# The transposes of the probabilities, moved to stand directly behind the scores on TensorE

## The reference, cut to what matters

```
x = x + scan_block(layernorm(x))             # a state-space scan with 16 states
x = x + cross_attention(layernorm(x), ctx)   # 32 heads of 128
x = x + ffn(layernorm(x))                    # one 512 x 512 matrix and low-rank terms
```

```
h  = layernorm(x);  hn = rmsnorm(h) * ln_weight
q, k, v = hn @ w_q.T, ctx @ w_k.T, ctx @ w_v.T
score = q k^T + position_bias[h]          # masked keys: minus infinity
prob  = softmax(score)
out   = (prob v) @ w_out.T                # summed over the 32 heads
result = h + out
```

## Time and profile before

| | us |
|---|---|
| median of 3 runs | 909.33 (909.28 to 910.69) |
| the profiled execution, its own time | 907.23 |
| its span, first to last instruction | 905.4 |
| TensorE busy | 896.5 (99%) |
| VectorE busy | 694.7 (77%) |
| GpSimd busy | 670.8 (74%) |
| ScalarE busy | 520.2 (57%) |

### The profile page before, as it was taken

How to read it: one execution, slowest core, us unless ns; L and a number is a source line. 1 busy time by engine, 2 the same in 40 slices (tenths; PEclk the granted TensorE clock), 3 DMA queues, 4 the chain that set the end, 5 groups by cost and what they waited for, 6 DMA issues and landing times.

```text
span 905.4 us, 15443 instructions
## 1 busy us (share of the span) xinstructions
PE 896.5 (99%) x5146; PEld 776.4 (86%) x5146; DVE 694.7 (77%) x757; ACT 520.2 (57%) x1198; POOL 670.8 (74%) x437
## 2 busy tenths in 40 slices
PE   8999999999999999999999999999999999999998
PEld 7687888788888888888899999999899999999876
DVE  4799899999999997475666767676667676767774
ACT  3787867665666765456555555555555555555330
POOL 3245989997678795566788787888987878787522
PEclk9999999999999999999999999999999999999999
DMA  9454767576686762457445444444454544444302
GB/s 304 174 168 146 201 200 207 185 216 207 193 281 191 240 198 96 145 172 243 161 147 161 137 158 143 152 146 153 131 166 135 160 136 160 140 156 138 98 1 94
DMA packets 96913, 150.32 MB, mean 166 GB/s; under 512 B 10608, under 2 KB 35312, under 8 KB 96736
## 3 DMA queue, kind: packets, MB, share of 16 engines
q1 hardware_dynamic: 86496, 131.60, 44.4%
q10 hardware_dynamic: 10368, 18.09, 7.7%
HBM read 113.88 MB, written 35.78 MB: 165 GB/s over the span
## 4 chain that ended last, share of the span: by engine, by line
PE 85%; POOL 7%; DVE 4%; issue 2%; DMA 1%; ACT 1%; SPq 0%; ACTq 0%; DVEq 0%; POOLq 0%
PE acc L522 10%; PE acc L524 10%; PE acc L523 10%; PE misc L522 6%; PE misc L523 6%; PE misc L524 6%; PE acc L754 6%; PE acc L809 6%; PE acc L686 5%; PE acc L688 5%; PE acc L687 5%; PE acc L778 3%; POOL y L1538 2%; POOL wv_lo L1500 2%; DVE misc L1268 1%
## 5 line engine op out<-in xcount | busy, mean ns | idle before, releaser
L1538 POOL TENSOR_TENSOR y<-y,w 128x2048 f32<-128x2048 f32 x31 | 143.5, 4629 | 34.9 <-DVE w L1275 31.1
L1268 DVE TENSOR_TENSOR_SCAN misc<-dA,misc 128x2048 f32<-128x2048 f32 x32 | 141.7, 4429 | 4.9 <-ACT dA L881 1.7
L1120 ACT ACTIVATE prob<-prob,negm 128x128 f32<-128x128 f32 x256 | 99.9, 392 | 43.6 <-DVE negm L1336 43.6
L1127 ACT ACTIVATE ot_hi<-acc 128x512 fp32r<-128x512 f32 x64 | 38.3, 599 | 143.5 <-PE acc L809 143.5
L1602 POOL TENSOR_TENSOR wt_lo<-ws,wt_hi 128x1024 fp32r<-128x1024 f32 x27 | 65.2, 2414 | 61.6 <-ACT wt_hi L1108 59.4
L522 PE MATMUL misc<-wo_hi,ot_hi 128*128 128x512 f32 x256 | 107.3, 419 | 0.0
L522 PE MATMUL acc<-wv_hi,ctx_hi 128*128 128x512 f32 x256 | 100.4, 392 | 1.4 <-POOL wv_lo L1500 1.4
L524 PE MATMUL misc<-wo_hi,ot_lo 128*128 128x512 f32 x256 | 101.2, 395 | 0.0
L523 PE MATMUL misc<-wo_lo,ot_hi 128*128 128x512 f32 x256 | 101.1, 395 | 0.0
L1619 POOL TENSOR_TENSOR wo_lo<-wo_raw,wo_hi 128x512 fp32r<-128x512 f32 x64 | 95.9, 1499 | 6.3 <-ACT wo_hi L1084 6.3
L524 PE MATMUL acc<-wv_hi,ctx_lo 128*128 128x512 f32 x256 | 99.8, 390 | 0.0
(11 more groups left out here) (206 smaller groups left out, 2448.2 us busy)
## 6 DMA issues: line engine op xcount, KB each, us to landing
k_scratch<-kst SPq DMA_DIRECT2D x64, 256.0 KB, 3.7
bc<-xp_scratch ACTq DMA_DIRECT2D x32, 512.0 KB, 5.6
v_scratch<-vst SPq DMA_DIRECT2D x32, 512.0 KB, 3.6
k_sb<-k_scratch SPq DMA_DIRECT2D x64, 256.0 KB, 2.7
v_sb<-v_scratch SPq DMA_DIRECT2D x64, 256.0 KB, 2.7
wo_raw<-in_wo SPq DMA_DIRECT2D x64, 256.0 KB, 2.9
wp<-in_wq SPq DMA_DIRECT2D x54, 256.0 KB, 3.7
wraw<-in_wk SPq DMA_DIRECT2D x32, 256.0 KB, 4.8
```

The costliest lines, as they stand in the source:

```text
L1120: last = act.activation(prob[q][:, b], prob[q][:, b], ACT.Exp, bias=negm[q][:, b:b + 1], accum_out=psum[q][:, b:b + 1])
L1268: dve.tensor_tensor_scan(h_ps, flat(dA[k % 2][:, :, :, :]), h_ps, 0.0, ALU.mult, ALU.add).then_inc(da_free, 1)
L1538: pool.tensor_tensor(y_half(half), y_half(half), w[:, k % 2], ALU.add).then_inc(y_ready, 1)
```

## The change

In TensorE's `step` the block with the transposes (with its two waits) moves from behind the products S1 and W11 to directly behind the scores. No instruction is added or taken away, and no other engine's program differs.

```diff
@@ in step(g, par, half, i) of the tensor engine @@
                     mm.then_inc(s_done, 1)
+                if runs(g - 2):
+                    pe.wait_ge(p_ready, g - 1)
+                    if known(g) and g == 2:
+                        pe.wait_ge(sum_evac, slot(NG, 0) - 1)
+                    else:
+                        pe.wait_ge(ot_lo_done, g - 2)
+                    for b in range(HB):
+                        mm = pe.transpose(psT[:, b * S:(b + 1) * S], prob[p][:, b], ident[:])
+                    mm.then_inc(t_done, 1)
                 if paired(i) and not p:
                     pe.wait_ge(c11_done, count(i))
                     product(sumX, S1, pp, *t_of(half, T1), True).then_inc(p5_done, 1)
                 if p and paired(i + 1):
 ...
                     pe.wait_ge(wa_lo, count(i) + 1)
                     product(sumX, W11, 1 - pp, *z_of(of, 0, 0), True).then_inc(p1_done, 1)
-                if runs(g - 2):
-                    pe.wait_ge(p_ready, g - 1)
-                    if known(g) and g == 2:
-                        pe.wait_ge(sum_evac, slot(NG, 0) - 1)
-                    else:
-                        pe.wait_ge(ot_lo_done, g - 2)
-                    for b in range(HB):
-                        mm = pe.transpose(psT[:, b * S:(b + 1) * S], prob[p][:, b], ident[:])
-                    mm.then_inc(t_done, 1)
                 if known(g) and STEPS <= g <= STEPS + 1:
```

## The result

| | before | after |
|---|---|---|
| median of 20 runs each, us | 909.07 (907.12 to 910.91) | 910.72 (909.14 to 912.68) |
| span of the profiled execution, us | 905.4 | 909.0 |
| first product with v, start of its first weight load in the trace, us | 392.95 | 394.81 |
| last product with v, the same, us | 871.31 | 874.90 |
| between these two, us | 478.36 | 480.09 |

The ratio is 1.0019, 95% interval 1.0011 to 1.0026, so 1.0 to 2.4 us slower. The forecast was 911.7, 2.3 us slower than the 909.33 it started from.

The account below looks back on a forecast made before the run. TensorE, busy 896.5 of 905.4 us, was taken as the bound. Its own work changing by 0, 26 waits of 0.09 us add 2.3 to 909.33: 911.7 us, own range 910.6 to 913.2, 8-in-10 range 909.8 to 914.0.

Parts of the forecast that it names:

- TensorE's own work: TensorE's matmuls in the new order: 0 to 0.5 us faster over 54 steps, taken as 0.
- Rival 3: f32/fp32r changes on TensorE really cost 0.08 us; 54 blocks save 4.3 us, less 2.3 of waits: 907.3 us; 5%.
- seams: Places on TensorE where one kind of matmul block follows another; claimed to cost 0.00 to 0.01 us each.
- Even steps: Transposes ahead of S1 in 27 steps: `ot_lo` is done 0.85 us earlier, so no wait.
- A wait for `ot_lo` in 26 odd steps: Transposes ahead of W11, steps 11 to 61: each waits 0.09 us for `ot_lo`, 2.3 us together.
- The three terms: One odd-step wait: `ot_lo` late 0.03, its end to the load 0.11, less 0.05 free: 0.09 us.
- What W11's delay triggers: W11 ends 0.53 us later, ScalarE's exponentials start 0.08 later; no second wait at S2.
- a thin margin at c21: Free time between `c21_done` and S2's load: 0.07 us, staying about 0.08 as TensorE itself arrives 0.09 later.
- Rival 2: Exponentials slip more than TensorE, `c21_done` misses S2 in each even step: 912.4 to 919.2 us, middle 915; 10%.
- The reaction to a semaphore: From `ot_lo`'s end to the transposes' load: 0.11 us taken, 0.05 kept as lower end; the skill gives 50-100 ns.

Follow-up runs that it names:

- e1: Kernel before with the transposes moved directly behind the scores in even steps alone; odd steps keep them behind W11. Ratio to the kernel before 0.9998.
- e5: Changed kernel with `ot_lo` computed in four pieces of 128 columns. Ratio to the kernel before 1.0067.
- e3: Changed kernel with the wait for `p_ready` moved ahead of the scores, so the transposes' first load waits for `ot_lo` alone. Ratio to the kernel before 1.0014.
- e8: Changed kernel with the transposes' two waits in the other order, `ot_lo_done` first and `p_ready` second. Ratio to the kernel before 1.0000.
- e7: Changed kernel with the W11 block moved ahead of the scores in odd steps. Ratio to the kernel before 1.0005.
- e9: Changed kernel with GpSimd's `wo_lo` put ahead of its `bm`. Ratio to the kernel before 1.0027.
- e2: Kernel before with the transposes moved directly behind the scores in odd steps alone; even steps keep them behind S1. Ratio to the kernel before 1.0027.

## Why the prediction was right

The mechanism and the place were right; the size was 0.6 us too large. The time, 910.72, lies 1.0 us below the forecast and just inside its own range of 910.6 to 913.2: 0.3 of this is the kernel before, whose median came out at 909.07 and not 909.33. The forecast gave "slower by over 0.2%" 0.58 and "within 0.2%" 0.36; the ratio of 1.0019 is narrowly in the second.

- **TensorE's own work, taken as 0.** Right to 0.01 us: e1 shows 0.006 to 0.013 us won in each even step, 0.28 us in all, inside the 0 to 0.5 that was kept as a bound. Rival 3, dear seams, is out by the same run.
- **Even steps have 0.7 us and more of cover.** Right: e1 loses nothing, and e5 makes `ot_lo` 0.19 us later without a loss there.
- **A wait for `ot_lo` in 26 odd steps.** Right in place and count. The three terms: `ot_lo` late by 0.03 (measured 0.026 in the first steps, 0.034 later); from its end to the load 0.11 (0.115, and e3 and e8 show that 0.06 of it is the order of the waits); 0.05 of a late load free (the second transpose 0.17 behind the load, 0.22 in a dense stream). An odd step grew by 0.078 to 0.101 us, forecast 0.09; 26 of them by 2.34, forecast 2.3.
- **What made the total smaller than forecast**, 1.73 and not 2.3 in the trace: the 0.3 us of the seams, taken as 0, 0.3 us given back where TensorE had waited before and now arrives later, and 0.07 in step 9. The last two were not in the sum at all.
- **What W11's delay triggers.** Nothing, as forecast. The first links held: the copy of W11 came 0.53 us later (forecast 0.53) and the exponentials 0.08 (forecast 0.08). But the margin at the end was kept by something that the prediction did not have, so that part was luck. It passed ScalarE's 0.08 us on through the normalisation with its length fixed, to a thin margin at c21. In fact the normalisation's end, and c21 behind it, was tied to the end of GpSimd's `bm`. Step 31 after, answering to the earlier trace rows: `bm` ends at 616.06 and the normalisation 0.56 us later, at 616.62; c21 ends at 617.01 and S2's load comes 0.155 us behind it, where it was 0.117 before. The normalisation takes 1.37 us and not 1.44. In most even steps the load comes 0.155 behind c21 (0.11 to 0.13 before); with 0.05 for the wait, the free time before S2 rose from 0.07 to 0.10 us.

```profile
614.90 1.16 POOL L1615 TENSOR_TENSOR bm<-bias,maskadd 128x512 f32<-128x512 f32 x1
...
615.25 1.37 DVE L1360 TENSOR_TENSOR prob<-prob,rec 128x512 f32<-128x512 f32 x1
616.59 0.42 DVE L1369 TENSOR_TENSOR q_sb<-acc,q_s 128x256 f32<-128x256 f32 x1
...
617.17 0.19 PEld L686 LDWEIGHTS acc<-tz,wt_hi 128*128 128x128 f32 x1
```

Rival 2 was priced with a length of VectorE that can't be carried over; e7, which delays the exponentials by 0.7 us at no cost, shows the margin to be far from thin on that side.
- **The reaction to a semaphore.** With the late wait on the load itself the runs show 0.053 us, with it in the second place 0.115. The Trainium skill (Advanced Engine Details and Errata, Network/Comms) gives 50-100 ns: the first agrees, the second lies just outside, and the row of the same instruction was the better guide.

## What to carry to other kernels

Before a consumer is moved ahead on a saturated engine, look at when its last input is ready against the new place, to the hundredth: cover of 0.7 us was worth nothing beyond the first 0.1, but its absence was paid 26 times. Of two waits on one load, write first the one that comes last, and check in the trace that it is on the load itself; here that alone was worth 1.4 us of the stretch. Do not carry an instruction's length from one order to another where its end goes with that of another engine's instruction.

## What the hardware showed that I had not expected

- VectorE's `prob * rec`, which reads and writes SBUF alone, starts beside a GpSimd instruction and ends 0.55 us behind the end of that one. This held to 0.01 us in before, after, e5, e7 and e9 wherever a GpSimd TENSOR_TENSOR had over 0.15 us left, with lengths from 0.72 to 1.81 us; with no GpSimd instruction running when it started it took 0.69. The one GpSimd instruction of another kind that was met, a TENSOR_SCALAR on 128x4 elements (L1476, `var<-mv`, step 63, 0.75 us), did not hold it: 0.69 us. A GpSimd instruction that began well within the hold did not prolong it. In e2 and e3, where the running one had 0.04 us left at the start and the next began within 0.01 us (step 36), the end came 0.55 behind that next one. What the two engines share was not tested.
- The order of two waits on one matmul's load changes its start behind the later one from 0.115 to 0.053 us (e8). The trace's records show why: the wait written last stands as an instruction of its own ahead of the load.
- A dip of the granted clock to 0.50 for 3.4 us, far ahead of the changed part, moved the profiled span by 1.7 us, as much as the whole effect.
- Late weight loads of transposes are partly free: in the 26 odd steps 0.05 us of the lateness did not reach the matmul.
